# Weights split once and fetched from DRAM, a value bias moved into the context, an epsilon summed as a square, and side products ordered after the scores

## What is computed

```python
xn = layernorm(x)
q  = rope(rmsnorm(xn @ Wq + bq, qn_w))                  # per head
lk = rope(rmsnorm(xn @ Wlk + blk, kn_w))
lv = xn @ Wlv + blv
w_cmp   = softmax((xn @ Wcmp + bcmp) in groups of 4 tokens)
entries = sum over each group of w_cmp * xn              # 256 entries per batch
ck = rope(rmsnorm(entries @ Wk + bk, kn_w)); cv = entries @ Wv + bv
# sparse branch: top 8 of the causal entries for each query, softmax, values cv
# local branch: softmax over a window of 128 keys back (own block and the one before), values lv
merged = (ctx_sparse + ctx_local) * 0.5
out = x + merged @ Wo + bo + fp8-rounded(xn) @ fp8-rounded(input2)
```

## Time and profile before

| | |
|---|---|
| median of 3 runs | 2707.45 us (2703.29 to 2707.54) |
| the profiled execution | 2711.33 us, span of its instructions 2709.2 us |
| PE busy | 2569.0 us, 95% of the span |
| DVE / ACT / POOL busy | 2066.4 / 1611.6 / 1855.2 us |
| DMA | 136.86 MB, 51 GB/s on average |

### The profile page before, as it was taken

How to read it: one execution, slowest core, us unless ns; L and a number is a source line. 1 busy time by engine, 2 the same in 40 slices (tenths; PEclk the granted TensorE clock), 3 DMA queues, 4 the chain that set the end, 5 groups by cost and what they waited for, 6 DMA issues and landing times. The chain is left out here.

```text
span 2709.2 us, 55203 instructions
## 1 busy us (share of the span) xinstructions
PE 2569.0 (95%) x15368; PEld 2242.8 (83%) x15368; DVE 2066.4 (76%) x6505; ACT 1611.6 (59%) x4433; POOL 1855.2 (68%) x3044
## 2 busy tenths in 40 slices
PE   4799999999999999999999999999999999999999
PEld 3688888888888888888888888888888888888887
DVE  5688787788877778777877778777787777777776
ACT  2555565556565656566666556656565666666665
POOL 3576666676688667666677867666766776667664
PEclk9899999999999999999999999999999999999999
DMA  3101110111232111111133111111113211110100
GB/s 103 44 28 44 48 48 28 42 42 48 71 102 65 46 48 48 34 42 44 48 98 102 40 47 44 48 48 48 32 58 101 81 36 33 34 35 24 32 25 32
DMA packets 150372, 136.86 MB, mean 51 GB/s; under 512 B 14258, under 2 KB 114100, under 8 KB 150068
## 3 DMA queue, kind: packets, MB, share of 16 engines
q1 hardware_dynamic: 150068, 133.33, 16.0%
HBM read 106.02 MB, written 27.26 MB: 49 GB/s over the span
## 5 line engine op out<-in xcount | busy, mean ns | idle before, releaser
L1226 POOL TENSOR_TENSOR t<-raw,tB 128x128 f32<-128x128 f32 x512 | 230.4, 472 | 373.4 <-DVE raw L832 371.3
L1180 POOL TENSOR_TENSOR r<-ss,mh 128x4 f32<-128x4 f32 x256 | 287.1, 1122 | 245.3 <-DVE ss L851 240.3
L454 PE MATMUL bQK<-wh,xh 128*128 128x512 f32 x1024 | 428.6, 419 | 0.8 <-DVE raw L832 0.8
L455 PE MATMUL bQK<-wl,xh 128*128 128x512 f32 x1024 | 406.5, 397 | 0.0
L456 PE MATMUL bQK<-wh,xl 128*128 128x512 f32 x1024 | 404.0, 395 | 0.0
L713 ACT ACTIVATE ch<-bVC 128x256 fp32r<-128x256 f32 x256 | 98.2, 384 | 481.5 <-PE bVC L528 480.8
L677 ACT ACTIVATE raw<-raw,r 128x128 f32<-128x128 f32 x512 | 177.9, 394 | 258.8 <-POOL r L1180 257.6
L879 DVE CUSTOM_DVE_ANT_0 P<-bS,cst 128x256 f32<-128x256 f32 (+1 forms) x512 | 203.3, 397 | 158.2 <-PE bS L502 156.1
L470 PE MATMUL bVC<-wh,xh 128*128 128x256 f32 x1024 | 310.4, 303 | 3.9 <-DVE cl L927 3.9
L1215 POOL TENSOR_SCALAR P<-P,rs 128x256 f32<-128x256 f32 (+1 forms) x512 | 286.7, 560 | 20.2 <-POOL P L1202 11.0
L683 ACT ACTIVATE P<-P,nm,r 128x256 f32<-128x256 f32 (+1 forms) x512 | 294.5, 579 | 0.0
(11 more groups left out here) (153 smaller groups left out, 7372.6 us busy)
## 6 DMA issues: line engine op xcount, KB each, us to landing
wr<-in_Wq SPq DMA_DIRECT2D x128, 128.0 KB, 2.4
wr<-in_Wlk SPq DMA_DIRECT2D x128, 128.0 KB, 2.8
wr<-in_Wlv SPq DMA_DIRECT2D x64, 256.0 KB, 3.1
wr<-in_Wo SPq DMA_DIRECT2D x64, 256.0 KB, 2.6
out<-acc SPq DMA_DIRECT2D x32, 256.0 KB, 2.9
ini<-in_hidden_states SPq DMA_DIRECT2D x24, 256.0 KB, 3.3
xs<-xsh SPq DMA_DIRECT2D x24, 256.0 KB, 2.6
xs<-xsl SPq DMA_DIRECT2D x24, 256.0 KB, 3.0
```

Source lines behind the costliest of these rows:

```text
L454: e.matmul(bQK[:, :], a, b, start=kt == 0, stop=False)
L455: e.matmul(bQK[:, :], a, bl, start=False, stop=False)
L1180: e.tensor_tensor(r4[:, u % 4], ss[:, u % 4], mh[:, 0:4], ALU.pow).then_inc(S["r4"], 1)
```

## The change

In four parts.

1. **Split weights kept.** After a split in batch 0, SP copies the high and low part of each chunk to DRAM (`keep`, `keep_wo`). The chunks of groups 8 to 31 are no longer loaded and split; SP fetches the ready halves straight into `wh`/`wl` (`fetch_w`) and `woh`/`wol` (`fetch_wo`).
2. **Value bias.** `blv_out` and `bias_row` are gone. `hi_c` and `lo_c` add blv/2 to the context instead, as a bias per partition, so each is now two instructions (one per head).
3. **Epsilon.** `sq` has a 129th column which holds it; `sum_qk` sums 129 values and `eps_qk` is gone.
4. **Order on PE.** `scores` stands ahead of `ckv`, `entries` and `ffn`.

```diff
@@ weight_chunks
-    for s in range(NU):
+    for s in range(64):
...
-        if i != 4 and i != 7 and gi + 1 < NU // 8:
+        if i != 4 and i != 7 and gi + 1 < NG:
@@ run_sync
+            def keep(gi, c):
+                e.wait_ge(S["split"], w_index(gi, c) + 1)
+                for n, half in enumerate(w_halves(gi, c)):
+                    e.dma_start(kept_of(gi, c, n), f32(half)).then_inc(S["d_k%d" % (gi % 2)], 16)
+            def keep_wo(gi, c):
+                e.wait_ge(S["wolo"], o_index(gi, c) + 1)
+                e.dma_start(kepto[gi, c, 0], f32(woh[:, c, :])).then_inc(S["d_ko"], 16)
+                e.dma_start(kepto[gi, c, 1], f32(wol[:, c, :])).then_inc(S["d_ko"], 16)
+            def fetch_w(gi, c):
+                if c == 0:
+                    e.wait_ge(S["qk"], 8 * (gi - 1))
+                    e.wait_ge(S["v"], 8 * (gi - 1))
+                    for w in range(2):
+                        e.wait_ge(S["d_k%d" % w], KEPT * NG // 2)
+                landed = S["d_%s%d" % ("q" if c < 4 else "v", gi % 2)]
+                for n, half in enumerate(w_halves(gi, c)):
+                    e.dma_start(f32(half), kept_of(gi % NG, c, n)).then_inc(landed, 16)
+            def fetch_wo(gi):
+                e.wait_ge(S["wo"], 8 * gi)
+                e.wait_ge(S["d_ko"], 16 * 4 * NG)
+                for c in range(2):
+                    e.dma_start(f32(woh[:, c, :]), kepto[gi % NG, c, 0]).then_inc(S["d_h"], 16)
+                    e.dma_start(f32(wol[:, c, :]), kepto[gi % NG, c, 1]).then_inc(S["d_h"], 16)
@@ run_sync, loop
+                if 64 <= s < NU and s % 8 == 5:
+                    fetch_wo(s // 8)
...
+                for kind, gi, c, split_at in CHUNKS:
+                    if kind == "w" and max(split_at, 0) + 2 == s:
+                        keep(gi, c)
+                    if kind == "o" and split_at + 1 == s:
+                        keep_wo(gi, c)
+                if s >= 56 and s % 8 < 6 and s // 8 + 1 < NU // 8:
+                    fetch_w(s // 8 + 1, s % 8)
@@ run_tensor, loop
+                if u2 is not None:
+                    scores(u2, 0)
+                    scores(u2, 1)
                 if block_at(s, "kv") is not None:
                     ckv(block_at(s, "kv"))
                 if tile_at(s, "et") is not None:
                     entries(tile_at(s, "et"))
                 if ffn_at(s, 3) is not None:
                     ffn(ffn_at(s, 3))
-                if u2 is not None:
-                    scores(u2, 0)
-                    scores(u2, 1)
...
-                if 0 <= s < 64 and s % 8 == 6:
-                    blv_out(s // 8)
@@ run_scalar
-                e.activation(pair(ch[:, u % 2]), bVC[:, 256:512], ACT.Copy).then_inc(S["hi_c"], 1)
+                for h in range(2):
+                    last = e.activation(ch[:, u % 2, h, :], bVC[:, 256 + h * 128:384 + h * 128], ACT.Identity,
+                                        bias=bias_of(u, h))
+                last.then_inc(S["hi_c"], 1)
@@ run_vector
-            def eps_qk(u):
-                e.wait_ge(S["sqs"], u + 1)
-                e.tensor_scalar(ss[:, u % 4], ss[:, u % 4], RMS_EPS, None, ALU.add, ALU.bypass).then_inc(S["veps"], 1)
...
-                e.tensor_tensor(pair(cl[:, u % 2]), bVC[:, 256:512], f32(pair(ch[:, u % 2])),
-                                ALU.subtract).then_inc(S["lo_c"], 1)
+                for h in range(2):
+                    last = e.scalar_tensor_tensor(out=cl[:, u % 2, h, :], in0=bVC[:, 256 + h * 128:384 + h * 128],
+                                                  scalar=bias_of(u, h), in1=f32(ch[:, u % 2, h, :]), op0=ALU.add,
+                                                  op1=ALU.subtract)
+                last.then_inc(S["lo_c"], 1)
...
-                    e.tensor_copy(blh[:, :], blT[:, :]).then_inc(S["blh"], 1)
-                    e.wait_ge(S["blh"], 2)
-                    e.tensor_tensor(bll[:, :], blT[:, :], f32(blh[:, :]), ALU.subtract).then_inc(S["bl"], 1)
```

More of the change, by code:

```diff
@@ L37 @@
 SIGNALS = (
-    "tr qk v s pt c wo xt bc et kv ct ff bw "
+    "tr qk v s pt c wo xt bc et kv ct ff "
     "kscale hi_qk p sq el es put_v hi_c wohi hi_x b8 ew put_et css hi_ck c8 "
-    "lo_qk rs raw t1 krest veps add ngr mc m8 ttr mr nm lo_c acc wolo bs ba xv xn wl wlb dg lo_x "
-    "eg neg re wtok wm init cke cm crest cadd cks lo_ck blh bl bo2 rsc isc wk tab rs0 "
+    "lo_qk rs raw t1 krest add ngr mc m8 ttr mr nm lo_c acc wolo bs ba xv xn wl wlb dg lo_x "
+    "eg neg re wtok wm init cke cm crest cadd cks lo_ck bl rsc isc wk tab rs0 "
     "r4 rstd ckp norm t2 sh split bo bo0 ones newck old e8 s8 sub sqs qb qd qs qn q8 "
[1 row of a table removed]
[1 row of a table added]
     "d_r0 d_r1 d_r2 d_r3 d_r4 d_r5 d_r6 d_r7 "
@@ L272, in mask_of, with w_halves, kept_of, weights_there @@
             return cst[:, a:a + nloc(u)]
-        def w_parts(q):
-            _, gi, c, _ = CHUNKS[q]
-            w, src = gi % 2, wr[:, q % 2, :]
+        def w_halves(gi, c):
+            w = gi % 2
             if c < 4:
-                return wh[:, w, c, 0:512], wl[:, w, c, 0:512], src
+                return wh[:, w, c, 0:512], wl[:, w, c, 0:512]
             k0 = 2 * (c - 4)
-            return (wh[:, w, k0:k0 + 2, 512:768], wl[:, w, k0:k0 + 2, 512:768],
-                    src.rearrange("p (k n) -> p k n", k=2))
+            return wh[:, w, k0:k0 + 2, 512:768], wl[:, w, k0:k0 + 2, 512:768]
+        def kept_of(g, c, n):
+            return kept[g, c, n] if c < 4 else kept[g, c, n].rearrange("p (k n) -> p k n", k=2)
+        def weights_there(e, gi, parts):
+            if gi < NG:
+                e.wait_ge(S["split"], w_index(gi, parts[-1]) + 1)
+            else:
+                e.wait_ge(S["d_%s%d" % ("q" if parts[0] == 0 else "v", gi % 2)], 32 * len(parts) * (gi // 2 - 3))
+        def wo_there(e, gi):
+            if gi < NG:
+                e.wait_ge(S["wolo"], o_index(gi, 1) + 1)
+            else:
+                e.wait_ge(S["d_h"], 64 * (gi - NG + 1))
         def run_sync(e):
@@ L448, in proj_qk @@
                     if i == 0:
-                        e.wait_ge(S["split"], w_index(gi, 3) + 1)
+                        weights_there(e, gi, (0, 1, 2, 3))
                     x_there(u)
@@ L464, in proj_v @@
                 if i == 0:
-                    e.wait_ge(S["split"], w_index(gi, 5) + 1)
+                    weights_there(e, gi, (4, 5))
                 x_there(u)
@@ L595, in ffn @@
                 free["Y"] = ("init", ffn_pos(t) + 1)
-            def blv_out(g):
-                e.wait_ge(S["wolo"], o_index(g, 1) + 1)
-                e.wait_ge(S[free["Y"][0]], free["Y"][1])
-                if g == 0:
-                    e.wait_ge(S["bl"], 1)
-                for h in range(2):
-                    a, al = (w[:, 2 * g + h:2 * g + h + 1].broadcast_to([128, 128]) for w in (blh, bll))
-                    e.matmul(bY[:, :], a, woh[:, h, :], start=h == 0, stop=False)
-                    e.matmul(bY[:, :], a, wol[:, h, :], start=False, stop=False)
-                    last = e.matmul(bY[:, :], al, woh[:, h, :], start=False, stop=h == 1)
-                last.then_inc(S["bw"], 1)
-                free["Y"] = ("bo2", g + 1)
             e.wait_ge(S["d_c"], 16 * 5)
@@ L668, in squares @@
                     e.wait_ge(S["sqs"], u)
-                e.activation(pair(sq[:, :, :]), flat(raw[:, u % 2]), ACT.Square).then_inc(S["sq"], 1)
+                e.activation(sq[:, :, 0:128], raw[:, u % 2].rearrange("p a b c -> p (a b) c"), ACT.Square).then_inc(S["sq"], 1)
             def kscale(u):
@@ L1131, in run_vector @@
                     sum_qk(u0)
-                    eps_qk(u0)
                     rope_add(u0)
```

36 lines of the change are left out of this document (20 added, 16 removed), and 2 rows, old and new, of the table SIGNALS.

## The result

The changed kernel takes 2620.47 us (median of 4 runs, 2619.43 to 2621.21) where the one before takes 2705.37 in the same session: ratio 0.9689, 95% interval 0.9672 to 0.9707. The forecast was 2625, with 2606 to 2656 as its range. The profiled execution took 2621.21 with a span of 2619.4, 89.8 less than the span of before.

The account below looks back on a forecast made before the run. PE, busy 95% of the span, bounds the kernel; 233 us lie above its matmul floor. Gains sum to 83.0, less one for the last steps: 82 off 2711.3 gives 2629.3, less 3.9 for the median, say 2625; range 2606 to 2656.

Parts of the forecast that it names:

- seven bias steps: Steps with `blv_out` from step 8 on: its 48 matmuls and the waits around them go, gain 25.8 us.
- entries: Steps with entries products: scores moved ahead fill PE's wait for `add_out`; excess 55.2 becomes 30.3, gain 24.9 us.
- ffn: Steps with feed-forward products alone: scores ahead remove most waits; excess 37.5 becomes 26.9, gain 10.6 us.
- ckv with ffn: Six steps with compression and feed-forward products: only ckv's own wait of 1 us in three steps goes, gain 3.0 us.
- plain steps: Steps without side product: no splits or Wo halves after batch 0, gain 11.8 of 12.9 us.
- turn: Steps with `turn_x` and logits: only steps 93 and 157 gain, about 1.7 us each, 3.4 in all.
- steps 2 to 7: Start of batch 0: weight waits half covered 2, `blv_out` 1.5 and some clock, first-key wait minus 1; gain 3.5 us.
- last steps: End of the kernel: `hi_c` stands in a chain that nothing covers, so one us is taken off the gain.
- More than the sum: Rival: remaining waits of turn steps and entries go too, down to 2600 us, likely 2610; chance 0.10.
- the reading of step 103: Entries step, 14.0 us against a clean 9.5: a wait of 1.8 us costs 3.6, as the granted clock falls.
- `kscale` has 3.5 us of cover: Norm chain in a clean step: `kscale` ends 3.5 us before `tr` starts, so coming 0 to 0.3 later costs nothing.
- The rival is real in one step, 69: Rival at the weight fetch: the Wo halves land late in 24 groups, costing 29 us, so 2654; chance 0.12.

Follow-up runs that it names:

- no_bias: The changed kernel with the bias products back in batch 0 and a single copy of the context again; 2636.83 us, ratio 0.9735.
- no_order: The changed kernel with the scores back behind the compression products, the entries and the feed-forward products; 2634.05 us, ratio 0.9726.
- two_orders: The changed kernel with feed-forward products behind the values in the six compression steps and scores last again in steps 2 to 7; 2614.97 us.
- pool_reads: The changed kernel with two idle POOL instructions reading SBUF (the reading pair) where the splits of batches 1 to 3 stood; 2629.06 us.
- the two kernels with idle pairs: The changed kernel with two idle POOL instructions where the splits of batches 1 to 3 stood, reading SBUF (2629.06 us) or only writing (2626.51 us).
- best_of_both: The changed kernel with feed-forward behind values in compression steps, scores last in steps 2 to 7, and `lo_x` ahead of the masks in batch 0; 2618.53 us.
- no_kept: The changed kernel with the kept weights undone, so that all 32 groups load and split again; 2643.81 us, ratio 0.976.
- kept_alone: The kernel before with only the split weights written to DRAM in batch 0 and fetched in batches 1 to 3; 2659.93 us, ratio 0.983.

## Why the prediction was right, and where it was not

The time was 2620, 5 under the forecast of 2625. For the profiled execution the forecast gain was 82 us and the measured one 90. By the excess of the steps, with `blv_out`'s seven steps kept apart, the gains came to this, in us:

| | forecast | measured |
|---|---|---|
| seven bias steps | 25.8 | 21.6 |
| entries | 24.9 | 34.2 |
| ffn | 10.6 | 12.5 |
| ckv with ffn | 3.0 | 4.8 |
| plain steps | 11.8 | 10.2 |
| turn | 3.4 | 7.8 |
| steps 2 to 7 | 3.5 | -1.0 |
| last steps | -1.0 | -2.0 |
| before step 2 | none | 1.9 |
| sum | 82 | 90 |

The total is nearer than its terms, and that is luck: four terms were too high, by 11 us together, four too low and one left out, by 19. Another 3 us met by chance: the forecast took 3.9 off the profiled execution for the median, and it was 0.7. What came on top of the sum is what the rival "More than the sum" names, the rest of the waits before the entries and in the turn steps; it came almost in full in batches 1 and 2, while the bias term and steps 2 to 7 fell 8.7 us short.

The signs came out as forecast: no longer clean steps, no wait of `out_proj` for a DMA, 6.3 us before the entries (under 12) and 5.3 before ffn (about 5), the pair `hi_c` at 0.62 (0.7), and steps 70 and 71 at 18.6. One is mixed: the idle time before `tr` fell as a whole, but in step 15 1.99 us of it appeared where there had been none.

**The entries.** The step that was sized wrong is what the order would leave behind in batches 1 and 2: 24.0 us, of which 14.4 for the matmuls, 5.6 for five short waits per batch and 4 for the lower clock. Measured were 14.7, the matmuls alone; batch 0 kept 6.3 as forecast. With the order alone 21.4 are left there. The kept weights and epsilon took the rest: taken out of the changed kernel, they bring 2.9 and 1.0 us back, the bias edit nothing (14.5). The forecast gave these two no share in the entries.

**The order** was sized well: alone it took 42.2 us off the three classes (27.5 + 10.0 + 4.7) where the terms say 38.5. Behind it stood the reading of step 103: a wait of 1.76 us costs more than itself. Eight entries steps of before, with waits of 1.31 to 1.76 us, had the lowered clock; step 117, with a wait of 1.52, had not. The price of such a fall can be read where the wait is the same. Step 15 in the changed kernel:

```profile
230.54:243.21 12.67, 10.58 (x66) 9.01 (x65) 12.19 (x40) 10.13 (x27) 9.32 (x14) 1.00 0.41 130
```

and in the kernel with reading instructions, which are not yet there in batch 0:

```profile
231.08:245.35 14.27, 12.17 (x67) 10.33 (x66) 13.07 (x41) 10.36 (x27) 10.93 (x15) 0.88 0.42 137
```

PE waits 1.99 and 2.01 us. The step is 1.60 longer with the fall. With an equal wait it came in one run and not in the other.

**The kept weights.** The step that failed is "the other turn waits stay, since ACT's three copies and DVE's `lo_x` are untouched". The instructions are untouched, the queue ahead of them is not: in batches 1 and 2 the turn steps fell from 21.9 to 11.3 us, to their matmuls (0.64 to 0.73 each, but for 0.98 in step 136). The term for plain steps, 11.8, was 10.2 (their excess before is 13.7 in the table above, not 12.9). Steps 70 and 71 take 18.62 as forecast. The reason given for them, POOL with two jobs at once, was in part wrong: with the reading pair POOL has both jobs again and the two steps have 0.65 of excess, against 3.3 without kept weights.

**The bias products.** The term 25.8 was 21.6 in the seven steps (30.3 to 8.7), and 2.8 went back into the other turn steps of batch 0. The step that failed is a wait taken as removed that moved on: step 14's wait had covered step 15's, which rose from 0.79 to 3.20. The rival is that the second instructions of `hi_c` and `lo_c` made DVE's `lo_x` late. In no_bias, with the products back and single copies, step 15 does not wait at all, and steps 8 and 36, which no bias step stands right before, wait 1.20 and 1.25 us in place of 1.19 and 1.34: so the second instructions cost 0.1 there at most, but no run has them beside the products. The pair `hi_c` is 0.62 us here, and clean steps did not get longer, as forecast.

**Epsilon.** Costed at nothing, since `kscale` has 3.5 us of cover. That looked at one reader of the chain. DVE is a queue, and `add_out` stands behind `eps_qk` in it. In step 103 `add_out` starts 2.48 us after the step's start in the kernel before (1164.34) and 1.84 after it with epsilon alone (1153.06):

```profile
1166.82 0.68 DVE L941 TENSOR_TENSOR acc<-bY,acc 128x512 f32<-128x512 f32 x1
```

```profile
1154.90 0.68 DVE L939 TENSOR_TENSOR acc<-bY,acc 128x512 f32<-128x512 f32 x1
```

That is 0.64 earlier, the whole of what the wait before the entries lost (1.76 to 1.11). Of it 0.20 is `eps_qk`'s own place in this step; the other 0.44 is there already at `sum_qk` ahead of it, carried over from the step before. Alone the edit was worth 21 us, in company 11.4.

**Steps 2 to 7.** Forecast 3.5 shorter, measured 1.0 longer; with the old order there they are 4.1 (no_order) and 4.3 (two_orders) shorter than in the changed kernel. The prediction had the mechanism, the scores of step 2 waiting for the first keys, and sized it at 1; the excess of step 2 alone rose from 10.27 to 12.81. The end of the kernel took 2 us more, where 1 was allowed; in pool_reads, with the same last steps, it took 0.3 more, so the 2 are no fixed price of the longer chain.

**The fetches** cost nothing in clean groups. In steps 228 and 229, PE's last use of the old Wo, SP's four issues and PE's first use of the new:

```profile
2334.17 0.40 PE L602 MATMUL bY<-woh,cl 128*128 128x512 f32 x1
...
2334.60 0.33 SPq L358 DMA_DIRECT2D woh<-kepto  x1
...
2335.91 0.43 SPq L359 DMA_DIRECT2D wol<-kepto  x1
...
2342.00 0.48 PE L600 MATMUL bY<-woh,ch 128*128 128x512 f32 x1
```

The page of the changed kernel gives the landings (KB each, median us from issue):

```profile
woh<-kepto SPq DMA_DIRECT2D x48, 256.0 KB, 3.4
wol<-kepto SPq DMA_DIRECT2D x48, 256.0 KB, 3.8
```

The slowest of that group landed 4.4 us after its issue, at about 2340.3 (2335.91 + 4.4), 1.7 before the use; 2.5 had been forecast. Over all 24 groups the last half landed 5.3 to 6.5 us after the first issue and 0.7 to 6.0 us before its use, so at its smallest the slack was 0.7. The estimate from the Trainium skill's 6.15 us for 1 MB (DMA: Bandwidth & Descriptors, section "Bandwidth") had put the end 8.2 us after the issue. That row is for DMAs issued from GpSimd, and these are issued by SyncE; the trace has 5.7 after the first issue here (2340.3 - 2334.60) and decides. The rival is real in one step, 69: there `out_proj` waited for `wol`, 1.41 and 1.28 us in the two kernels with idle pairs, 1.29 in no_bias, 0.81 with the kept weights alone and 0.35 in best_of_both. POOL adds the output's bias in these steps, and SP's store of `acc`, which needs that sum, stands ahead of `fetch_wo` in its queue; with the reading pair SP issued it 0.5 us after step 69 had begun, in the changed kernel 1.5 us before. In best_of_both SP was as early as in the changed kernel, and the halves took 7.5 us to land in place of 6.3. The changed kernel does not wait there.

**The parts do not add up.** Alone they took 34, 45, -1 and 21 us off, 99 together; taken back from the changed kernel they cost 14, 23, 16 and 11, 65 together; all at once are worth 85. The order, the kept weights and epsilon each removed the same entries waits: 27.5, 22.0 and 18.7 us of entries alone, 34.2 together. The bias edit is worth something only once the others have made room.

## What to carry to other kernels

A wait of 1.3 to 2 us after which the granted clock fell cost about twice itself here, so an edit of 0.3 us in the queue of the engine that is waited for can be worth 20 us, and a part measured alone says little about its worth beside others. When an instruction is removed, go through all that stands behind it on its engine and ask who waits for it, not only its own reader; when a wait is removed, ask which later wait it covered. How much work an engine loses says little about the gain: POOL busy for 1.9 us more in three steps of four cost PE 2 us in 128 steps.

## What the runs showed of the hardware

- A DVE instruction of 0.16 us with two SBUF operands took 1.21 to 1.22 us when it started 0.1 us after a POOL instruction of 1.29 us that reads SBUF, and at most 0.17 in all 96 cases beside one of POOL's idle fills. It goes the other way too: in all 29 cases of no_kept a POOL instruction of 0.48 us took 1.43 beside DVE's split of Wo, which reads two SBUF operands and had started first.
- The granted clock fell after a wait of 2.01 us in one run and not after 1.99 in another, and in one trace after 1.33 but not after 1.34; one fall cost 1.6 us. From step 8 on, no step of any trace had a lowered clock without a wait of 1.25 us or more in it (step 139 of kept_alone has the shortest), and step 29 of before waited 3.15 at the full clock. So the length of a wait alone did not settle it.
- Four DMAs of 256 KB issued within 1.8 us, two each for `woh` and `wol`, had all landed 5.3 to 6.5 us after the first issue in the 24 groups of the changed kernel.
